# A four-layer decoder on one core: norms moved into the two narrow attentions, state-space weights prepared one stage earlier, a bf16 split of the decay attention's shares, and a reordered last quad

## What is computed

```
# L0 attention: 16 heads of 8, projected q/k/v, softmax times a decay matrix
# L1 attention: the same shape without projections
q = x * rotation_params; k = x * entangle_params; v = x
attn_weights = softmax(q @ k.T * scale); out = attn_weights @ v
# L1 feed-forward, then L2 attention (a state-space scan, "mamba"):
x_conv = silu(conv(x @ W_in) + conv_b)
h = exp(dt * A) * h + (dt * x) * B;  y = sum(h * C)          # A = -exp(A_log)
# L2 feed-forward (fp4-rounded operands), then L3 attention (8 heads of 64):
attn = softmax(einsum('bhd,bhd->bh', q_t, k_t) * scale, axis=-1)   # over the heads
new_state = decay * state + (1.0 - decay) * attn[..., None] * v_t
out = layernorm((q * states + sigmoid(q * aug_param)) @ Wo + bo) * ln_scale + ln_bias
# L3 cross-attention (RWKV): sigmoid(r) * wkv, with r = layernorm(x)
# L3 feed-forward: a mixture of 14 experts, the best two weighted
result = clip(x + w0 * out0 + w1 * out1, -100, 100)
```

## Time and profile before

| what | value |
|---|---|
| median of 3 runs | 1676.36 us (1675.87 to 1677.19) |
| the profiled execution | 1684.5 us |
| its span, first to last instruction | 1682.3 us |
| busy in the span | PE 88%, PEld 57%, DVE 70%, ACT 53%, POOL 43% |
| granted TensorE clock, mean | 0.947 |
| stages, us from the span's start | loads to 11.5; L0 attention to 170; mLSTM and first experts to 320; L1 attention to 440; L1 cross-attention to 675; L1 feed-forward to 729; state space to 1024; L2 cross-attention to 1245; L2 feed-forward and L3 attention to 1446; experts to 1682 |

### The profile page before, as it was taken

One profiled execution on the slowest core, in us unless ns is written; L12 is line 12 of the kernel. 1 busy time (PEld: TensorE's weight loads), 2 busy tenths in 40 slices (PEclk: granted clock), 3 DMA queues, 4 the chain that ended last, 5 costly groups with the idle time before them and its releaser, 6 DMA issues. The chain is left out here.

```text
span 1682.3 us, 28868 instructions
## 1 busy us (share of the span) xinstructions
PE 1474.7 (88%) x9987; PEld 951.8 (57%) x9987; DVE 1173.6 (70%) x2554; ACT 898.8 (53%) x2612; POOL 724.9 (43%) x690
## 2 busy tenths in 40 slices
PE   4998787699799999978899888999977886879998
PEld 2565554455577765543334327888854443557776
DVE  4988567589687856538998887777767795644443
ACT  2765342377677752226776755777743443434443
POOL 2657453222664432217889893323441244341000
PEclk9999898899999999988999999999988997889999
DMA  7000000000000000020000000000000000000000
GB/s 294 1 2 1 1 2 1 1 1 2 1 2 2 2 1 1 1 90 1 1 1 1 1 1 2 2 2 2 2 1 0 1 1 0 1 1 7 8 7 7
DMA packets 3167, 18.98 MB, mean 11 GB/s; under 512 B 592, under 2 KB 720, under 8 KB 2256
## 3 DMA queue, kind: packets, MB, share of 16 engines
q1 hardware_dynamic: 3024, 17.14, 2.5%
HBM read 16.09 MB, written 1.05 MB: 10 GB/s over the span
## 5 line engine op out<-in xcount | busy, mean ns | idle before, releaser
L827 POOL TENSOR_TENSOR l_xattn_probs<-l_xattn_probs,l_xattn_recip 128x512 f32<-128x512 f32 x128 | 133.3, 1042 | 222.7 <-DVE l_xattn_recip L766 222.2
L999 ACT ACTIVATE l_attn_probs<-ps,l_attn_neg_max 128x128 f32<-128x128 f32 x512 | 145.1, 384 | 72.7 <-DVE l_attn_neg_max L1048 71.1
L2630 POOL TENSOR_TENSOR l_mamba_hc<-l_mamba_h,l_mamba_c 128x512 f32<-128x512 f32 x128 | 159.2, 1271 | 0.0
L2532 DVE TENSOR_TENSOR_SCAN l_mamba_h<-ps,l_mamba_dBx 128x512 f32<-128x512 f32 x128 | 152.5, 1210 | 1.9 <-ACT ps L2429 0.7
L2302 PE MATMUL ps<-l_mamba_hc,w_const 128*128 128x512 f32 x256 | 136.5, 637 | 19.6 <-POOL l_mamba_hc L2630 16.5
L3295 DVE SCALAR_TENSOR_TENSOR xn<-ps,l_gates,xn 128x128 f32<-128x128 f32 x224 | 63.0, 343 | 116.9 <-PE ps L2940 116.7
L761 DVE COPY l_xattn_probsT<-ps 128x512 f32<-128x512 f32 x128 | 87.9, 687 | 70.8 <-PE ps L613 70.8
L3075 ACT ACTIVATE wkv<-ps,w_early 128x512 f32<-128x512 f32 x112 | 70.8, 684 | 114.4 <-PE ps L2929 114.2
L2940 PEld LDWEIGHTS ps<-w_early,wkv 128*128 128x128 f32 x896 | 109.0, 194 | 28.6 <-issue 18.7
L2940 PE MATMUL ps<-w_early,wkv 128*128 128x128 f32 x896 | 111.1, 277 | 8.8 <-ACT wkv L3075 8.8
L712 ACT ACTIVATE l_xattn_probs<-ps,l_xattn_neg_max 128x128 f32<-128x128 f32 x256 | 91.9, 390 | 41.3 <-DVE l_xattn_neg_max L756 41.3
(11 more groups left out here) (531 smaller groups left out, 3634.5 us busy)
## 6 DMA issues: line engine op xcount, KB each, us to landing
w_early<-in_l_moe SPq DMA_DIRECT2D x1, 3669.0 KB, 11.8
w_l_xattn<-in_l_xattn SPq DMA_DIRECT2D x1, 2176.0 KB, 22.2
w_early<-in_l_xattn SPq DMA_DIRECT2D x1, 1890.0 KB, 14.6
w_l_attn<-in_l_attn SPq DMA_DIRECT2D x1, 1242.0 KB, 24.8
ctx<-in_ctx SPq DMA_DIRECT2D x1, 1088.0 KB, 10.5
x<-in_x SPq DMA_DIRECT2D x2, 512.0 KB, 4.2
ctxT<-in_ctxT SPq DMA_DIRECT2D x1, 1024.0 KB, 8.4
out_x<-x SPq DMA_DIRECT2D x4, 256.0 KB, 2.7
```

The source lines that it names most:

```text
L827: nc.gpsimd.tensor_tensor(probs[:, D % 2, n, :, :], probs[:, D % 2, n, :, :], along(recip[:, D % 2, n, :], [P, HALF, P]), ALU.mult).then_i ...
L999: ins = nc.scalar.activation(probs[:, t % 4, g, :], S_of(t)[:, g * P:(g + 1) * P], ACT.Exp, bias=neg_max[:, t % 2, g:g + 1], accum_out=total)
L2532: nc.vector.tensor_tensor_scan(flat(h[:, t % 2, half, :, :]), G.ps[:, DA_BANK[half], :], flat(dBx[:, t % 2, half, :, :]), 0.0, ALU.mult, A ...
L2630: nc.gpsimd.tensor_tensor(heads4(hc[:, t % 4, half, :]), h[:, t % 2, half, :, :], c_sb[:, t % 3, :, :], ALU.mult).then_inc((hc0_set, hc1_s ...
```

## The change

1. **Start.** SP issues only x (two halves), const and the L0 attention's weights before the first barrier; the other 12 are issued in the attention's block (`load_rest`). The first block does the statistics of x on DVE and the first power on POOL.
2. **Narrow attentions.** Both lose their `layernorm` block and take a `Lead`. In `l1_attn` PE also gets 30 filler products (`keep_clock`).
3. **State-space weights** (`MambaWeights`) are prepared within `l1_ffn`; `l2_mamba` takes a `Lead` instead of the norm block. PE gets 14 fillers at the feed-forward's end and 11 at the state space's start.
4. **Shares of the L3 attention** are split into three bf16 parts on DVE; PE turns and spreads them in bf16 (`probs3`, `spread3`).
5. **Order in the last block.** `add_down`, `normals`, POOL's `attended_normals` for the last quad go ahead of the scans; `receptance(0)` and `receive(0)` move from before the exponential of quad 2 to after its chunks; `project(LAST)` from before `second(0, 0)` to after it; `receptance(LAST)` from expert 5 to expert 9; `below_max(0)` ahead of `apply`; `received_spreads(LAST)` from (0, 10) to (1, 1).

```
+def keep_clock(nc, G, bank, n):
+    for _ in range(n):
+        nc.tensor.matmul(G.ps[:, bank, :], G.ident_bf[:], G.mask_kq_bf[:].unsqueeze(1).broadcast_to([P, 4, P]), start=True, stop=True)
...
 narrow_attention, PE
+            lead.needs(pe)
+            lead.tensor(pe, 0)
             if projected:
                 project(0)
+                pe.wait_ge(consts, 1)
                 pe.wait_ge(p_taken, 1)
+            lead.tensor(pe, 1)
+            if not projected:
+                keep_clock(nc, G, X_BANK, 10)
             for t in range(STEPS + OUT_LAG + 1):
                     scores(t)
+                if not projected and t < OUT_LAG:
+                    keep_clock(nc, G, X_BANK, 5)
...
+                if t < 2:
+                    lead.tensor(pe, 2 + t)
...
 l1_ffn, PE, down(q)
+                if q == NQ - 1:
+                    pe.wait_ge(gelued, CH * q + 3)
+                    kept.spread_taps(pe, (1, 2))
...
+                if q == NQ - 2:
+                    pe.wait_ge(gelued, CH * (q + 1) + 1)
+                    kept.turn_taps(pe, 0)
...
+            keep_clock(nc, G, 3, 14)
 l1_ffn, DVE
+                if q == NQ - 2:
+                    kept.fixed(dve)
                 if q == NQ - 1:
+                    kept.vector(dve, (1, 2))
                     ahead.apply(dve, nc.vector, 5)
 l2_mamba, PE
+            lead.tensor(pe, 0)
+            keep_clock(nc, G, 5, 5)
+            lead.wait(pe, 0)
                 convolve(0, half, tap)
+            lead.tensor(pe, 1)
+            keep_clock(nc, G, 4, 6)
             x_bc(0)
...
 l2_ffn_and_l3, ACT
-                if q > 1:
+                if q == LAST:
                     receptance(q - 2)
...
+                if q == LAST - 1:
+                    receptance(0)
...
                     if (q, e) == (0, 0):
+                        exponentials(0)
+                    if (q, e) == (0, 1):
                         take_out(LAST)
-                        exponentials(0)
                     if (q, e) == (0, 5):
                         receptance(LAST - 1)
+                    if (q, e) == (0, 9):
                         receptance(LAST)
...
 DVE, shares(q)
-                nc.vector.tensor_tensor(probs[:], probs[:], along(top[:], [P, QUAD, H]), ALU.mult).then_inc(p_set, 1)
+                link(nc.vector.tensor_tensor(probs[:], probs[:], along(top[:], [P, QUAD, H]), ALU.mult))
+                for n in range(2):
+                    link(nc.vector.tensor_copy(probs3[:, :, n, :], probs[:]))
+                    link(nc.vector.tensor_tensor(probs[:], probs[:], probs3[:, :, n, :], ALU.subtract))
+                nc.vector.tensor_copy(probs3[:, :, 2, :], probs[:]).then_inc(p_set, 1)
```

More of the change, by code:

```diff
@@ L851, in narrow_attention @@
     OUT_LAG = V_LAG + (2 if projected else 1)
+    first, G.started = not G.started, True
     with Scope(nc, G, tag) as s:
@@ L880, in narrow_attention, with _ @@
         by_head = lambda a, h: a.rearrange("p (h k) -> p h k", h=h)
+        @block.sync
+        def _(sp):
+            if first:
+                load_rest(nc, G, sp)
+            lead.sync(sp)
         @block.tensor
@@ L884, in project @@
             def project(b):
+                lead.wait(pe, b)
                 after(pe, p_taken, b)
@@ L1035, in seen @@
                     ahead.variances(dve)
+            lead.rest.early(dve, nc.vector, 0, 0)
+            dve.wait_ge(G.loaded["const"], 16)
+            if first:
+                small_constants(nc, G, dve).then_inc(consts, 1)
+            if prepare:
+                lead.needs(dve)
+                prepare(dve)
             heads = G.c["heads"].rearrange("p (r i) -> p i r", r=4)
@@ L1042, in _ @@
                 nc.vector.memset(v_sb[:, :, :, DH:DH + 1], 1.0).then_inc(masked, 1)
+            lead.rest.variances(dve)
+            for q in range(1, lead.rest.first // QUAD):
+                lead.rest.early(dve, nc.vector, 0, q)
+            lead.rest.late(dve, nc.vector, 0)
             for t in range(STEPS + OUT_LAG + 1):
@@ L1074, in keys @@
                 else:
+                    lead.wait(pool, b)
                     source = G.xnT[:, b, :]
@@ L1083, in keys @@
                     nc.gpsimd.tensor_copy(v_sb[:, b % 4, :, 0:DH], by_head(G.xn[:, b, :], H)).then_inc(v_set, 1)
+            lead.rest.early(pool, nc.gpsimd, 1)
             pool.wait_ge(masked, 2 if projected else 3)
-            keys(0)
+            if projected:
+                lead.rest.scales(pool)
+                lead.rest.late(pool, nc.gpsimd, 1)
+                keys(0)
+            else:
+                keys(0)
+                lead.rest.scales(pool)
+                lead.rest.late(pool, nc.gpsimd, 1)
             for t in range(STEPS + OUT_LAG + 1):
@@ L1350, in l1_ffn, with l1_ffn_and_l2_mamba @@
+def l1_ffn_and_l2_mamba(nc, G):
+    with Scope(nc, G, "l2_mamba_w") as s:
+        kept = MambaWeights(nc, G, s)
+        l1_ffn(nc, G, kept)
+        l2_mamba(nc, G, kept)
+def l1_ffn(nc, G, kept):
     w = G.w["l1_ffn"]
@@ L2216, in l2_mamba @@
         XD_BANK, DT_BANK, OUT_BANK, BC_BANK = 6, 6, 6, 7
+        lead = Lead(nc, G, s, "l2_mamba", (4, 5, 4, 5))
         ahead = Ahead(nc, G, s)
@@ L2221, in l2_mamba, with _ @@
         at = lambda t: (t // NS, t % NS)
+        @block.sync
+        def _(sp):
+            for group in EARLY:
+                sp.wait_ge(G.loaded[group], 16)
+            sp.dma_start(G.pack["l3_moe"], G.aps["l3_moe"]).then_inc(G.loaded["l3_moe"], 16)
+            lead.sync(sp)
         @block.tensor
@@ L2293, in start_sum @@
                 pe.wait_ge(xc_set, 2 * (q + 1))
+                lead.wait(pe, NB - 1)
                 after(pe, y_set, 2 * q)
@@ L2442, in copy_c @@
                 nc.scalar.copy(c_sb[:, t % 3, :, :], bank4(C_BANK)).then_inc(c_copied, 1)
-            act.wait_ge(taps_turned, 1)
-            nc.scalar.copy(taps[:], G.ps[0:2 * TAPS, 0, 0:P]).then_inc(taps_copied, 1)
-            nc.scalar.activation(ea[:].rearrange("p a n -> p (a n)"), w["a_log"], ACT.Exp).then_inc(ea_set, 1)
-            act.wait_ge(a_set, 4)
+            lead.scalar(act, 0)
             for half in (1, 0):
@@ L2567, in _ @@
             ins.then_inc(zeroed, 1)
-            link = Link(dve, own)
-            for n in range(2):
-                link.note(nc.vector.tensor_scalar(minus[:, n, :], G.c["ident"][0:3 * M, 0:3 * M], -1.0, None, ALU.mult))
-            link.catch()
-            for n in range(2):
-                ins = nc.vector.memset(minus[:, n, 0:M * (n + 1)], 0.0)
-            ins.then_inc(minus_set, 1)
+            lead.rest.variances(dve)
+            lead.rest.early(dve, nc.vector, 0)
+            lead.rest.late(dve, nc.vector, 0)
             branch_x(0, 1)
@@ L2699, in l2_ffn_and_l3 @@
         probs = s.sb("probs", [P, QUAD, H])
-        probsT = s.sb("probsT", [P, QT])
-        sel_e = full(G, "const", "sel_e")
+        probs3 = s.sb("probs3", [P, QUAD, 3, H], BF16)
+        probsT = s.sb("probsT", [P, QT], BF16)
+        spread3 = s.sb("spread3", [P, QT], BF16)
         v_sb = s.sb("v", [P, 2, QT])
@@ L2963, in _ @@
             first(0, 0)
-            for j in range(QUAD):
-                project(LAST, j)
+            first(0, 1)
             for q in range(NQ):
@@ L2969, in _ @@
                     if (q, e) == (0, 0):
-                        first(0, 1)
+                        for j in range(QUAD):
+                            project(LAST, j)
                     if e + 2 < E:
@@ L3463, in _ @@
             nc.gpsimd.memset(probsT[:], 0.0).then_inc(blank, 1)
+            nc.gpsimd.tensor_copy(spread3[:], full(G, "const", "sel_e")).then_inc(blank, 1)
             lead.rest.scales(pool)
@@ L3498, in _, with load @@
             received_normals(LAST)
-def load(nc, G, aps):
+def load(nc, G, aps, with_stats):
+    s = Scope(nc, G, "load")
+    begun = Ahead(nc, G, s, first=NB // 2) if with_stats else None
+    exponent = s.sem("exponent")
     @G.first.sync
```

203 lines of the change are left out of this document (135 added, 68 removed).

## The result

The changed kernel takes 1631.6 us (1630.9 to 1633.4, 4 runs) against 1676.1 us (1673.8 to 1677.2, 4 runs): 0.9738 of the time before, 95% interval 0.9725 to 0.9750, or 44.5 us less. The forecast was 1632. The profiled execution took 1631.55, its span is 1629.7, the granted clock 0.964 on average (0.947 before).

A forecast was written before the change was run, and what follows sets the result against it. PE, busy 88% of the span, was taken as the path, stage by stage, with POOL the path in the state space. Terms 6 + 5.5 + 8 + 25.0 = 44.5 off the median 1676.4 gave 1632 us; range 1619 to 1650.

The forecast's parts named there:

- A: Kernel start, L0 attention: fewer first DMAs and reordered statistics bring the first mask product to 19.5; gain 6 us.
- B: L1 attention's start: keys(0) needs only quad 0's norm, and fillers keep PE busy; gain 5.5 us.
- Rival 1: At the new starts, fillers don't hold PE's clock; B loses 4 and C 6 us, giving 1642; chance 0.17.
- C: State-space start: weights prepared within the feed-forward, power 2.1 us later, fillers hidden in PE's wait; gain 8 us.
- D1: L3 attention: reordering gains 9.5 us at quad 2; bf16 shares book +0.5, -1.0, +1.2 for quads 0, 1, 3; total 10.2.
- Rival 2: L3 attention: the split's five small DVE operations stretch to 1.09 us each beside POOL, giving 1638; chance 0.12.
- D2: Last quad's projection: two first and one second fill PE's 4.20 us wait for POOL's l_o; gain 4.4 us.
- D3: Experts: moving the last sigmoids four experts later removes PE's 8.80 us stall at expert 6; gain 10.4 us.
- Rival 3: Expert 9: a table switch costs twice what its row shows, PE stands 3 us, giving 1637; chance 0.05.
- Rivals 4 and 5: Scan falls into a slower rhythm, 1680; or the change doesn't do what it says, stall moving to expert 9, 1674; 0.03 each.

The follow-up runs named there:

- warm_fp32: The kernel of warm_again with the decay attention's shares in fp32 again instead of three bf16 parts: 1627.6 us, 0.9678 of the kernel before.
- warm_again: The changed kernel with POOL's keys(0) earlier and PE fillers added in the L0 attention, run as a control: 1634.5 us, 0.9713 of the kernel before.

## Why the prediction was right

The time (1632 for 1631.6) and the sum (44.5 for 44.5, and 43.4 in the traces at the edits' own places) came out; not every term did. Two things do not fit the sum: the 4.2 us at the mLSTM come with the change and stood in no term, and the last block alone gave 17 us where its terms are 25.

- **A, start.** 6 forecast, 5.9 in the trace; no run has it undone. The mask product came at 20.1 for 19.5. The chain was the right one: barrier, DVE, POOL's power, normals, `keys`.
- **B, L1 attention.** 5.5 forecast, 6.3 in the trace, 5.4 when undone. Rival 1, that the fillers don't hold the clock, is out: 0.99, and 0.64 without them.
- **C, state space.** 8 forecast, 9.4 in the trace, 16.6 when undone. The +2.1 ahead of the power, the hidden fillers and the convolution's length were as booked. The price of the old start differs by execution: I read the earlier trace rows as it was in one, with the convolution half cold; in another it was cold throughout, and more half clock followed in later stages.
- **D1, L3 attention.** 10.2 forecast, 5.1 in the trace; this step failed in part. Quad 2 gave 9.8 for 9.5, though what was late next was not the last chunk but ACT's copy of `xnT` behind `receptance(0)`. Quads 0 and 1 lost 2.8 for the booked 0.5, and quad 3 lost 1.9 (0.6 by POOL's `l_o`) where +1.2 was booked. The booking "the bf16 shares halve or better PE's turns and spreads" counted a shorter PE as a gain. The pair `warm_fp32` and `warm_again` shows the opposite: in front of a wait for POOL the shorter products gain no time, the five operations make POOL 1.1 us later, PE drops to half clock behind the longer wait, and undoing the split gives 6.9 us. On the base of the change itself the difference did not show. Rival 2 did not come true: of the 20 operations of the split one took 1.14 us, at quad 3, and the others 0.18 or 0.19 (the row of 1.07 is the product that took 1.09 before).
- **D2, projection.** 4.4 forecast, 6.8 in the trace (5.5 by POOL's `l_o`). The wait of 4.20 went as booked, but for 0.98 ahead of `second(0, 0)`; in addition the projection itself ran at full clock, 1.12 and 3.84 us for 2.07 and 6.12.
- **D3, stall.** 10.4 forecast, 9.9 in the trace, 12.4 when undone. The visit at expert 9 was priced at 4.2 and took 1.28 + 1.65 + 1.28 with 0.02 between, all inside ACT's slack. The cover was over-sized: gelus of the first quad come 3.50 us apart, so four experts are 14 us and not the 20 booked, which was enough for a chain 8 late. Rival 3 is out. The Trainium skill ("ScalarE: Activation LUTs", section "What ACT_TABLE_LOAD costs") adds a drain of about the load's own length to each switch; in this trace the activation starts 1.30 us after the load did.
- Rivals 4 and 5 did not occur: the scan's products on POOL have the same mean, 1.269 us for 1.271, and no idle time before them.

That D1's shortfall of 5 was made up by D2, C and B, by 4.6 in the traces, is luck; the range would have held without it. It is luck too that terms read from an execution 8 us long could be taken off the median as they stood.

## What to carry to other kernels

Read the start of each stage for who releases whom, and price the products behind a wait at the clock they will get. Before making PE's work shorter, ask what PE does next: ahead of a wait on another engine the time is not won, the hole can cost the clock behind it, and what makes the work shorter may stand in the queue of the engine that PE waits for. And put the sum against several executions: what stands in one profile of the kernel before and not in another (2.9 us here) belongs to no edit, and what stands in all profiles of the change may (4.2 us), even where the code is the same.
